# Graph network on one core: the edge MLP's attribute product in two short-float passes, its bias copied by ScalarE

## The reference

```python
def mish(x):
    return x * jnp.tanh(jax.nn.softplus(x))
edge_feat = jnp.concatenate([x[src], x[dst], edge_attr], axis=-1)   # 512 + 512 + 64
h = mish(edge_feat @ W1 + b1)
messages = mish(h @ W2 + b2)
agg = jax.ops.segment_sum(messages, dst, num_segments=x.shape[0])
```

## Time and profile before

| | |
|---|---|
| median of 3 runs | 1295.84 us (1293.26 to 1300.98) |
| the profiled execution | 1297.59 us, its span 1295.8 us |
| PE busy | 1214.3 us (94%) |
| PEld busy | 646.6 us (50%) |
| DVE busy | 795.6 us (61%) |
| ACT busy | 556.7 us (43%) |
| POOL busy | 510.5 us (39%) |
| costliest group | L1184, 696 matmul records, 315.1 us |
| L1167 (attribute product) | 696 records, 101.5 us |

### The profile page before, as it was taken

The page is one execution under the profiler, slowest core; times in us unless marked ns, Lnnn a source line. Parts: engine busy times, 40 slices in busy tenths (PEclk is TensorE's granted clock), DMA queues, the critical chain, the costliest instruction groups (busy, mean ns, idle before and its releaser), DMA issues. The chain is left out here.

```text
span 1295.8 us, 15266 instructions
## 1 busy us (share of the span) xinstructions
PE 1214.3 (94%) x4908; PEld 646.6 (50%) x4908; DVE 795.6 (61%) x1576; ACT 556.7 (43%) x975; POOL 510.5 (39%) x442
## 2 busy tenths in 40 slices
PE   7898899599999999899999999999999979899995
PEld 3433433244544444555555555555555546445552
DVE  5764564667322323267778777777778756846663
ACT  1021211210110211357777777777777733225552
POOL 1111111253242000277766666666666100047661
PEclk9999899799999999889999999999999989999998
DMA  8699686555400201496544444444444020036662
GB/s 342 230 342 362 236 316 247 180 185 166 175 15 8 95 1 43 117 221 154 109 94 94 95 97 92 96 91 98 92 96 82 1 68 1 17 123 201 185 183 79
DMA packets 59444, 175.86 MB, mean 136 GB/s; under 512 B 12485, under 2 KB 13029, under 8 KB 52584
## 3 DMA queue, kind: packets, MB, share of 16 engines
q0 software_dynamic: 32496, 76.65, 25.0%
q1 hardware_dynamic: 26872, 98.23, 20.9%
HBM read 160.32 MB, written 14.52 MB: 135 GB/s over the span
## 5 line engine op out<-in xcount | busy, mean ns | idle before, releaser
L1184 PE MATMUL PS<-w,hidT 128*128 128x512 f32 x696 | 315.1, 595 | 0.0
L542 POOL DMA_INDIRECT rec_scratch<-rec_src,slot_row x84 | 99.4, 1184 | 287.6 <-DMA rec_scratch<-rec_src,slot_row 234.1
L1184 PEld LDWEIGHTS PS<-w,hidT 128*128 128x128 f32 x696 | 132.3, 191 | 134.0 <-issue 126.7
L1007 POOL DMA_INDIRECT pair_sum<-table_i,counts_rec x87 | 87.4, 1004 | 219.1 <-POOLq L63 130.7
L1015 POOL DMA_INDIRECT pair_sum<-table_j,counts_rec x87 | 147.6, 1697 | 30.7 <-issue 26.2
L1119 ACT ACTIVATE grow<-PS 128x512 f32<-128x512 f32 x174 | 104.0, 598 | 119.1 <-PE PS L1167 83.9
L1280 POOL DMA_INDIRECT u_space<-table_j,rec x87 | 82.3, 946 | 130.8 <-DMA table_j<-agg_rows 94.1
L269 PE MATMUL PS<-is_src,is_dst 128*128 128x512 bf16 x420 | 111.6, 397 | 20.4 <-DVE is_src L575 19.3
L1124 ACT ACTIVATE grow<-grow,two 128x512 f32<-128x512 f32 x174 | 124.8, 717 | 5.0 <-DVE grow L1065 4.9
L1065 DVE SCALAR_TENSOR_TENSOR grow<-grow 128x512 f32<-128x512 f32 x174 | 120.6, 693 | 6.0
L317 PE MATMUL PS<-w_rel,hT 128*128 128x512 f32 x240 | 107.6, 605 | 13.6 <-DMA w_rel<-w_scratch 11.9
(11 more groups left out here) (216 smaller groups left out, 1795.2 us busy)
## 6 DMA issues: line engine op xcount, KB each, us to landing
ring<-basis_rows SPq DMA_DIRECT2D x48, 1024.0 KB, 7.4
ring<-basis_low SPq DMA_DIRECT2D x30, 512.0 KB, 4.6
w_scratch<-stage SPq DMA_DIRECT2D x96, 32.0 KB
rec_scratch<-ring POOLq DMA_DIRECT2D x2, 1496.0 KB, 14.8
counts_rec<-rec_scratch SPq DMA_DIRECT2D x1, 2992.0 KB, 10.7
rec_scratch<-rec_src,slot_row POOLq DMA_INDIRECT x168, 3.5
root<-L_gnn_root SPq DMA_DIRECT2D x2, 1024.0 KB, 7.8
w_rel<-w_scratch SPq DMA_DIRECT2D x1, 2048.0 KB
```

The costliest lines, as they stand in the source:

```text
L542: nc.gpsimd.indirect_dma_start(out=rec3_dram, out_offset=bass.IndirectOffsetOnAxis(ap=slot_row[:, 1, t:t + 1], axis=0), in_=rec, in_offset ...
L1007: nc.gpsimd.indirect_dma_start(out=pair_sum[:, t % GOT3, :], out_offset=None, in_=tables[0][0], in_offset=bass.IndirectOffsetOnAxis(ap=idx ...
L1184: m = nc.tensor.matmul(o, hidT[:, t % 2, k * P:(k + 1) * P], w2[:, k, :], start=False, stop=(k == KT - 1), skip_group_check=True)
```

## The change

The attributes are split in a high and a low short-float part, which stand in partitions 0 to 63 and 64 to 127 of `attr`; the weights are split the same way into two tiles `w_attr`, each holding its part twice, so that two short-float products over all 128 rows give all four cross products. The split of the attributes costs a subtraction on DVE per group of four tiles, ahead of the loop. The bias is broadcast to all partitions by its DMA, and ACT copies it into the message's bank, at the end of its step and behind a wait on `mish0`; PE's message waits for the new semaphore `bias`.

```diff
-            attr = sb("attr", [ED, SC * P], F32, p3)
-            w_attr = sb("w_attr", [ED, D], F32, p3)
+            attr = sb("attr", [P, SC * P], F32R, p3)
+            w_attr = [sb(f"w_attr{j}", [P, D], F32R, p3) for j in range(2)]
...
+            b2_all = sb("b2_all", [P, D], F32, p3)
...
-            pre_bank = lambda t: 5 + max(2 * t - 1, 0) % 3
+            pre_bank = lambda t: 5 + (2 * t - 1) % 3
...
 # sync
-                sp.dma_start(b2_in[:], a["b2_row"]).then_inc(sem("b2_in"), 16)
-                sp.dma_start(w_attr[:], a["L2_gnn_W1"][2 * D:2 * D + ED, :]).then_inc(sem("w_attr_in"), 16)
+                sp.dma_start(b2_all[:], a["b2_row"].broadcast_to((P, D))).then_inc(sem("b2_in"), 16)
+                for j in range(2):
+                    sp.dma_start(w_attr_in[ED * j:ED * j + ED, :], a["L2_gnn_W1"][2 * D:2 * D + ED, :]).then_inc(sem("w_attr_in"), 16)
...
 # vector, ahead of the loop (the bias split in three bf16 rows goes)
+                dve.wait_ge(sem("w_attr_in"), 32)
+                nc.vector.tensor_copy(w_attr[0][:], w_attr_in).then_inc(sem("w_attr_hi"), 1)
+                dve.wait_ge(sem("w_attr_hi"), 1)
+                nc.vector.tensor_tensor(w_attr[1][:], w_attr_in, w_attr[0][:].bitcast(F32), ALU.subtract).then_inc(sem("w_attr_lo"), 1)
+                for j in range(N_TURN):
+                    dve.wait_ge(sem("attr_T"), j + 1)
+                    nc.vector.tensor_tensor(attr[ED:P, j * D:(j + 1) * D], PS[0:ED, j % 8, :], attr[0:ED, j * D:(j + 1) * D].bitcast(F32),
+                                            ALU.subtract).then_inc(sem("attr_low"), 1)
...
 # scalar
+                def bias(t):
+                    act.wait_ge(sem("mish0"), t + 1)
+                    nc.scalar.copy(PS[:, mes_bank(t), :], b2_all[:]).then_inc(sem("bias"), 1)
...
                     if 0 <= s - 1 < NS:
                         high_part(s - 1)
+                    if 0 <= s + 1 < NS:
+                        bias(s + 1)
...
 # tensor, pre(t)
-                    if t == 2:
-                        pe.wait_ge(sem("mish0"), 1)
...
                     for k in range(KT):
-                        m = nc.tensor.matmul(PS[:, pre_bank(t), k * P:(k + 1) * P], w_attr[:, k * P:(k + 1) * P],
-                                             attr[:, t * P:(t + 1) * P], start=False, stop=True, skip_group_check=True)
-                        if k == 0 and t:
-                            bias(t - 1)
+                        for w in w_attr:
+                            m = nc.tensor.matmul(PS[:, pre_bank(t), k * P:(k + 1) * P], w[:, k * P:(k + 1) * P],
+                                                 attr[:, t * P:(t + 1) * P], start=False, stop=True, skip_group_check=True)
...
 # tensor, message(t)
-                    if t == NS - 1:
-                        bias(t)
+                    pe.wait_ge(sem("bias"), t + 1)
...
 # tensor, ahead of the loop
-                pe.wait_ge(sem("attr_T"), N_TURN)
+                pe.wait_ge(sem("attr_low"), N_TURN)
```

More of the change, by code:

```diff
@@ L960, in gnn_stack @@
             GOT3, LAG3, LATE5, HOT3, TURN_GROUP = 9, 3, 8, 2, 4
-            attr = sb("attr", [ED, SC * P], F32, p3)
-            w_attr = sb("w_attr", [ED, D], F32, p3)
+            attr = sb("attr", [P, SC * P], F32R, p3)
+            w_attr = [sb(f"w_attr{j}", [P, D], F32R, p3) for j in range(2)]
             w2 = sb("w2", [P, KT, D], F32, p3)
-            b2_in = sb("b2_in", [1, D], F32, p3)
-            b2_rows = sb("b2_rows", [P, D], BF16, p3)[ED:P, :]
-            ones = sb("ones", [P, P], BF16, p3)[ED:P, :]
+            b2_all = sb("b2_all", [P, D], F32, p3)
             pair_sum = sb("pair_sum", [P, GOT3, D], F32, p3)
@@ L973, in gnn_stack @@
             is_dst3 = sb("is_dst3", [P, HOT3, P], F32R, p3)
+            w_attr_in = hidT[:, 0, :]
             none = mes[:, 0, :].bitcast(BF16)[:, 0:D]
-            b2_flat = mes[0:1, :, :].rearrange("p b o -> p (b o)").bitcast(BF16)
-            b2_part = [b2_flat[:, (j + 1) * D:(j + 2) * D] for j in range(3)]
             idx = rec[:, :, 0:2].bitcast(I32)
-            pre_bank = lambda t: 5 + max(2 * t - 1, 0) % 3
+            pre_bank = lambda t: 5 + (2 * t - 1) % 3
             mes_bank = lambda t: 5 + (2 * t + 2) % 3
@@ L1046, in _ @@
             def _(dve):
-                nc.vector.memset(b2_rows, 0.0).then_inc(sem("b2_zero"), 1)
-                nc.vector.memset(ones, 1.0).then_inc(sem("b2_ones"), 1)
                 nc.vector.memset(none, 0.0).then_inc(sem("none"), 1)
[L1051 to L1057, removed]
+                dve.wait_ge(sem("w_attr_in"), 32)
[6 more added lines that the diff above has]
+                                            ALU.subtract).then_inc(sem("attr_low"), 1)
                 def grown(l, t):
@@ L1135, in high_part @@
                     nc.scalar.copy(mes_hi[:, t % 2, :], mes[:, t % 2, :]).then_inc(sem("mes_hi"), 1)
+                def bias(t):
+                    act.wait_ge(sem("mish0"), t + 1)
+                    nc.scalar.copy(PS[:, mes_bank(t), :], b2_all[:]).then_inc(sem("bias"), 1)
                 for j in range(N_TURN):
                     act.wait_ge(sem("attr_tp"), j + 1)
-                    nc.scalar.copy(attr[:, j * D:(j + 1) * D], PS[0:ED, j % 8, :]).then_inc(sem("attr_T"), 1)
+                    nc.scalar.copy(attr[0:ED, j * D:(j + 1) * D], PS[0:ED, j % 8, :]).then_inc(sem("attr_T"), 1)
+                act.wait_ge(sem("b2_in"), 16)
                 for s in range(-1, NS + 1):
@@ L1166, in pre @@
                     for k in range(KT):
-                        m = nc.tensor.matmul(PS[:, pre_bank(t), k * P:(k + 1) * P], w_attr[:, k * P:(k + 1) * P],
-                                             attr[:, t * P:(t + 1) * P], start=False, stop=True, skip_group_check=True)
-                        if k == 0 and t:
-                            bias(t - 1)
+                        for w in w_attr:
+                            m = nc.tensor.matmul(PS[:, pre_bank(t), k * P:(k + 1) * P], w[:, k * P:(k + 1) * P],
+                                                 attr[:, t * P:(t + 1) * P], start=False, stop=True, skip_group_check=True)
                     m.then_inc(sem("pre_mm"), 1)
-                def bias(t):
-                    pe.wait_ge(sem("mish0"), t + 1)
-                    nc.tensor.matmul(PS[:, mes_bank(t), :], ones, b2_rows, start=True, stop=False, skip_group_check=True)
                 def message(t):
                     chunk = None
-                    if t == NS - 1:
-                        bias(t)
+                    pe.wait_ge(sem("bias"), t + 1)
                     o = PS[:, mes_bank(t), :]
@@ L1205, in _ @@
                     if j >= 8:
-                        pe.wait_ge(sem("attr_T"), j - 7)
+                        pe.wait_ge(sem("attr_low"), j - 7)
                     for g in range(TURN_GROUP):
@@ L1214, in _ @@
                     nc.tensor.matmul(PS[:, c, :], none[:, 0:P], none, start=True, stop=False, skip_group_check=True)
-                pe.wait_ge(sem("w_attr_in"), 16)
+                pe.wait_ge(sem("w_attr_lo"), 1)
                 for s in range(-1, NS + 2):
-                    if s == 0:
-                        pe.wait_ge(sem("b2_ones"), 1)
-                        pe.wait_ge(sem("b2_rows"), 48)
                     if s == 1:
```

## The result

The changed kernel takes 1323.65 us (median; 1316.34 to 1336.67, 4 runs) against 1294.86 us before (1293.26 to 1300.98, 4 runs). The ratio is 1.020, its 95% interval 1.0153 to 1.0247: slower, and whether by more than 2% is left open. The profiled execution took 1324.03 us with a span of 1322.2 us, where that of before had 1297.59 and 1295.8. Single executions of this study came out long (1336.67 here, 1333.21 and 1342.99 of changed_again, 2547.26 of product_only, 4626.62 of early_short_start), and the ratios are taken without them, the medians with them.

The account below looks back on a forecast made before the run. TensorE was taken to set the 5.61 us period before, a ScalarE and VectorE ring after; 16.2 us from 85 tiles plus 4.7 at the start gave +20.9, hence 1317 us, range 1308 to 1360.

Parts of the forecast that it names:

- slower: Outcome that the changed kernel takes longer than before, covering the forecast and the dear-products rival; chance 0.86.
- The ring: Loop chain from bias copy through exp1, ScalarE and VectorE steps, hidT to next copy: 5.80 us against 5.61, +16.2 us.
- the other path: In the loop, via VectorE's one-hot, the other layer's clamp and top to ln0: at most 0.06 us longer.
- The start: Before the loop, weight split and 22 subtractions delay the first transposes by 5.7 us; net +4.7 after the first message.
- the saving of 0.95: At the loop's first message: it starts 1.37 us after the first hidT, where it started 2.32 after.
- TensorE's own sum: TensorE's work per tile in the loop after the change: 5.39 us, with 4.99 and 6.24 at the bounds.
- The rival of dear narrow products: Attribute product: a narrow short-float product costs 0.213 like f32, TensorE stays the bound at 6.24, 1354 us; chance 0.30.
- The faster rival: In the loop the ring does not bind and TensorE's saving comes through: period 5.39, 1282 us; chance 0.06.
- The signs: Mid-loop profile: period 5.80, copy waits for hidT, exp1 not for TensorE, TensorE idle some 0.4 a tile, products 0.86.

Follow-up runs that it names:

- changed_again: The changed kernel run once more without any edit: 1314.93 us against 1295.41 before, ratio 1.013; its profiled execution took 1342.99 us.
- product_only: The changed kernel's short-float product alone, with the bias added by a TensorE matmul as in the kernel before: 1313.70 us against 1293.73.
- early_short_start: copy_early with the start reordered, weights' DMAs first and the attribute subtractions ahead of the weights' split: 1288.78 us against 1317.56, ratio 0.977.
- copy_early: The changed kernel with ScalarE's bias copy moved to the next step, behind exp1 and ahead of exp0: 1273.48 us against 1293.73 before, ratio 0.983.
- copy_twice_late: The changed kernel with the bias copied twice at the end of the step, the second copy waiting for the first: 1384.79 us against 1317.56 before.
- bias_only: The changed kernel's ScalarE bias copy alone, with the f32 attribute product of the kernel before: 1309.92 us against 1293.73.
- early_f32_product: bias_only with the bias copy moved ahead of exp0, as in copy_early: 1309.47 us against 1317.56 before, period 5.62 us.

## Why the prediction was right

The time, 1323.65, lies in the range (1308 to 1360), 7 us above the 1317 forecast and inside the forecast's own 1309 to 1329; slower had 0.86. The second set of the same kernel lies 19.5 us above before (1314.93 against 1295.41), the first 28.8, where +20.9 was forecast: the 7 us are within what two sets differ by.

- *The ring and its direction.* Right, and confirmed from three sides: copy_early (take the copy out of the ring: 5.23), copy_twice_late (lengthen it by 0.63: +0.62), bias_only (the ring without the rest of the change: 5.76). Predicted 5.80, measured 5.75. Most of the 0.05 is ln0 after inv1: I read 0.58 in a row where ln0 in fact waited for the other path, top0 (806.67 to 807.40, the 0.73 of a hand-over), and it measured 0.54. Small parts are inv0 after ln0 (0.75, measured 0.73) and two of 0.01, and the copy's 0.53 instead of 0.50 offsets some. With 85 tiles the term was +16.2 predicted, +12.6 measured.
- *The start.* Named, and undersized: +4.7 predicted, +9.1 measured up to exp1 of tile 0. The part up to the first transposes is +8.2 instead of +5.7. The split of the weights began at 547.65, 6.7 us after the phase's first DMA, where I had put the landing 5.0 us after it; and the way from the last subtraction (562.06) past the clearing matmuls to the transposes took 2.2 instead of 1.2. The 22 subtractions came as costed, 13.23. At the first message the saving of 0.95 came almost whole: it starts 1.46 after hidT (570.29 to 571.75) instead of 2.32. But TensorE had been idle for 2.4 and 4.2 us in the start, and its granted clock was 0.50, the lower level (1.2 GHz), from 562 to 566.7, where before it was 1.00 from 549 to 552. That cost 1.0 in the clearing matmuls and 1.0 up to exp0 of tile 0, whose eight records took 1.92 us against 1.16, and the first message was 0.6 longer (granted clock 0.59 from 571.7 to 578). A price for the clock is the term that the forecast of the start lacks.
- *The two misses nearly cancel*: 16.2 + 4.7 = 20.9 predicted for the edge MLP; 12.6 + 9.1 and -0.8 behind the last period, 20.9, measured. That this agrees to a tenth is chance.
- *The rest of the 26.4 us between the traces* was spread ahead of the phase, which I had no second trace to see; that it did not carry the time out of the forecast's own range is luck too.
- *TensorE's own sum.* The forecast did not rest on it, but it was argued wrongly: the bias matmul, which I priced at 0.22, cost nothing where it was (early_f32_product). Its other misreading is the 0.107 for a pair, which is 0.112; the 1.08 are eight such pairs and 0.20 for the way out of the 64-row mode, and not 0.86 and 0.22. For the new order the prediction had 5.39 and copy_early measured 5.23: 0.36 instead of 0.53 from the transposes to the products, 0.52 instead of 0.57 in the segment sum, and 0.92 instead of 0.86 for the eight.
- *The rival of dear narrow products*, 0.30: refuted, 0.115 each in copy_early and not 0.213. *The faster rival*: its time, 1282, was about what the saving is worth (0.983 of before), but the copy could not give it where it stood; the step from hidT to exp1 measured 1.25, not under 1.04.
- *The signs.* The copy waits for hidT, exp1 waits for nothing, TensorE's gaps are put down to VectorE, and the granted clock stays 1.00 in the middle of the loop, all as named; the gaps sum to 0.30 a tile by the window, with 0.4 named.
- *What I did not see*: that the ring, once it sets the pace, can also run at 6.04, by where GpSimd's issues fall. The path that it then takes was priced at most 0.06 longer, with VectorE's operations at their quick durations.

## What to carry to other kernels

An engine that is a quarter idle is not free: its idle time lies in certain gaps, and an instruction costs nothing only in a gap whose wait is on someone else's late work, and only if its own wait is long met by then. Ahead of adding an instruction, follow who waits for what is queued behind it; a ring that returns to the instruction itself has a length that can be summed from start-to-start times in the old trace, to 1% here. Look also for the rings that come next: one by VectorE's one-hot (6.04) and one by the message (5.50) were each a few tenths away. One call moved by one place turned 2.0% slower (1.3% in the second set) into 1.7% faster.

## What the runs showed of the hardware

- VectorE's clamp and one-hot (both TENSOR_SCALAR) took 424 and 282 ns, or 547 and 432 ns, in two executions of one program, by where GpSimd's indirect DMA issues lay against them. Lying inside an issue is not enough: a clamp that started 0.36 us into a gather of 0.98 took 0.43 (803.43), one that started 0.65 into one of 0.99 took 0.59 (805.16). The Trainium skill ("SBUF — State Buffer", section Who interferes with whom) says that tensor_scalar in its two-port modes shares a port pair with GpSimd. The traces agree in that the tensor_scalar operations are hit most: the two-input L1058 went only from 693 to 718 ns, the two with one input in PSUM (L1065, L1080) not at all (688 ns in the one execution, 687 and 688 in the other).
- That contention can hold itself in place. The gather is released by TensorE's products, which follow the segment sum by a fixed amount of work (4.36 us in both traces), so a longer ring brings the gather earlier against the ring: 0.79 behind the copy at 5.75 a tile, 0.50 at 6.04. There the clamp falls on its end, and that keeps the ring long. The numbers are from the two traces; that this is what holds the ring at 6.04 is argued from them. It fits that the long ring ends with the last gather and that the run with the later gather did not show it.
- Eight 128-column short-float products on 128 rows take 0.92 us, the four f32 ones on 64 rows 1.09, with 0.17 more to enter them. Both are eight pairs of weight load and matmul at 0.112 from load to load; what differs is the way in and the way out.
- A copy of 128x512 f32 by ScalarE from SBUF into PSUM took 0.59 us and the next instruction started 0.53 after it; its cast from SBUF to SBUF took 0.60.
- The semaphore hand-over between ScalarE and VectorE was 0.03 to 0.04 us from the end of one row to the start of the waiting one (top1 ends at 804.58, ln1 starts at 804.62).
